# A vision tower on one core: the average's kernel made at the program's beginning, the gather written out over 128 rows, the places loaded in two pieces

## What is computed

```python
logits = jnp.einsum('bsd,de->bse', x, gate_weight)
affinity = jax.nn.softmax(logits, axis=-1).transpose(0, 2, 1)
gating, index = jax.lax.top_k(affinity, k)                       # k = 8 of 65 tokens
x_in = jnp.take_along_axis(x[:, None, :, :], index[..., None], axis=2)
h = jax.nn.gelu(jnp.einsum('bekd,edh->bekh', x_in, w1) + b1[None, :, None, :])
x_e = jnp.einsum('bekh,ehd->bekd', h, w2) + b2[None, :, None, :]
...
def step(h, xt):
    h = p_coeff[None] * xt[:, :, None] + q_coeff[None] * h
    return (h, jnp.sum(gamma[None] * h, axis=-1))           # scanned over the 65 tokens
...
w = jax.nn.softmax(adaptive_weights)
return w[0] * out_attn + w[1] * x_cema
```

## Time and profile before

| | us |
|---|---|
| median of 3 runs | 828.24 (827.29 to 828.71) |
| profiled execution, its own time | 827.36 |
| its span | 825.6 |
| TensorE busy (x8455) | 630.7 |
| VectorE busy (x904) | 504.3 |
| ScalarE busy (x871) | 348.7 |
| GpSimd busy (x254) | 230.8 |

### The profile page before, as it was taken

The page is one execution under the profiler, slowest core; times in us unless marked ns, Lnnn a source line. Parts: engine busy times, 40 slices in busy tenths (PEclk is TensorE's granted clock), DMA queues, the critical chain, the costliest instruction groups (busy, mean ns, idle before and its releaser), DMA issues. The chain is left out here.

```text
span 825.6 us, 21280 instructions
## 1 busy us (share of the span) xinstructions
PE 630.7 (76%) x8455; PEld 513.7 (62%) x8455; DVE 504.3 (61%) x904; ACT 348.7 (42%) x871; POOL 230.8 (28%) x254
## 2 busy tenths in 40 slices
PE   2999999999999996761399867858689999971002
PEld 1888888888888885541394546638567777761001
DVE  0376666666666666427222678759578888855862
ACT  0013444444444444422164333443167888865600
POOL 1263333333333333000000223330235555430001
PEclk9999999999999998665558997775579999995555
DMA  8443333333332300003980440000000000001300
GB/s 358 161 191 119 118 119 117 117 117 117 117 117 117 117 2 2 2 1 106 198 116 0 54 52 0 0 2 0 1 2 4 0 0 0 3 2 53 74 5 4
DMA packets 28659, 55.36 MB, mean 67 GB/s; under 512 B 12274, under 2 KB 25698, under 8 KB 26114
## 3 DMA queue, kind: packets, MB, share of 16 engines
q1 hardware_dynamic: 28515, 54.62, 22.1%
q0 software_dynamic: 96, 0.07, 0.0%
HBM read 48.14 MB, written 6.55 MB: 66 GB/s over the span
## 5 line engine op out<-in xcount | busy, mean ns | idle before, releaser
L375 PE MATMUL a_bank<-a_x,a_tok_w 128*128 128x256 f32 (+1 forms) x608 | 150.6, 390 | 15.7 <-DVE a_ht L555 15.7
L375 PEld LDWEIGHTS a_bank<-a_x,a_tok_w 128*128 128x128 f32 (+1 forms) x608 | 113.1, 192 | 37.3 <-DMA tables<-in_tables 15.7
L124 POOL TENSOR_TENSOR a_qt<-a_qp,data 128x512 f32<-128x512 f32 x64 | 71.8, 1153 | 2.1 <-POOL a_qp L617 1.6
L617 POOL TENSOR_TENSOR a_qp<-a_rope 128x260 f32<-128x260 f32 x16 | 11.7, 733 | 175.5 <-DVE a_rope L499 175.5
L282 ACT ACTIVATE a_at<-a_bank 65x256 f32<-65x256 f32 x128 | 38.9, 390 | 26.8 <-PE a_bank L259 26.8
L493 DVE SCALAR_TENSOR_TENSOR a_ht<-a_bank,data 128x256 f32<-128x256 f32 x16 | 7.7, 484 | 64.5 <-PE a_bank L375 64.5
L1449 POOL TENSOR_TENSOR b_e<-b_e,b_inv 128x585 f32<-128x585 f32 (+1 forms) x32 | 35.4, 1108 | 22.6 <-DVE b_inv L1299 22.6
L259 PE MATMUL a_bank<-a_mix,a_e 64*65 64x64 f32 x1024 | 41.5, 237 | 0.0
L259 PEld LDWEIGHTS a_bank<-a_mix,a_e 64*65 64x65 f32 x1024 | 36.9, 149 | 4.1 <-issue 3.4
L910 POOL COPY s_ycp<-yout 128x512 f32<-128x512 f32 (+1 forms) x16 | 11.5, 726 | 97.6 <-POOLq L829 93.5
L195 ACT ACTIVATE a_e<-a_e 128x390 f32<-128x390 f32 (+1 forms) x48 | 24.3, 510 | 33.2 <-DVE a_e L175 33.2
(11 more groups left out here) (251 smaller groups left out, 1520.2 us busy)
## 6 DMA issues: line engine op xcount, KB each, us to landing
a_x<-in_x SPq DMA_DIRECT2D x16, 2304.0 KB, 7.9
lag_rows<-r_kernel SPq DMA_DIRECT2D x1, 4192.5 KB, 38.8
lags<-lag_rows SPq DMA_DIRECT2D x1, 2112.5 KB
base<-places SPq DMA_DIRECT2D x1, 2080.0 KB
out<-e_plain SPq DMA_DIRECT2D x16, 130.0 KB
expert_weights<-in_w SPq DMA_DIRECT2D x2, 1024.0 KB, 5.9
a_tok_w<-in_tok_w SPq DMA_DIRECT2D x1, 1152.0 KB, 6.7
data<-in_data SPq DMA_DIRECT2D x1, 910.5 KB, 4.7
```

The costliest lines, as they stand in the source:

```text
L124: nc.gpsimd.tensor_tensor(qt[:, b * BLOCKS * P:(b + 1) * BLOCKS * P].rearrange("p (c h i) -> p c h i", i=qb, h=HEADS), wide(by_image[:, b, ...
L375: mm = nc.tensor.matmul(banks[0][:, 0:GP], w[0:rows, k * DIM:(k + 1) * DIM], x[p][0:rows, k * GP:(k + 1) * GP], start=(k == 0), stop=(k == ...
```

## The change

1. **The average's kernel.** `prepare_average` is split. Its first part, now `average_kernel`, stands at the head of VectorE's program of the first block, behind a wait for `data` alone (`S.data_in`, which takes the place of one half of `S.setup`) and ahead of the wait for the tables. SP stores `lag_rows` at the end of its program of the first block, behind the last load of `x`, and waits for it there. The rest, `blend_of_branches`, stays in the second block; the two operations on `adapt` and that on `wo_bv` move behind the subtraction of the peak.
2. **The gather.** `R.h_tok` gets 128 partitions; GpSimd clears partitions 64 to 127 at the program's beginning, and row 64 is written again with every group. TensorE reads `h_tok` itself, so the copies to `tok` go. There are four `pick` of 128 partitions, whose upper 64 GpSimd clears in the second block and of which VectorE writes 65, and four PSUM banks. The loops are written out. The product is 128 rows by 128 columns instead of 65 by 128; what is added is zero.
3. **The places.** SP waits for `places` only, and loads `place_all` for groups 0 to 3 and then for groups 4 to 15. Only then it stores `gates`, and reads both back into `rows`. TensorE turns `rows` behind the gather instead of ahead of it, and VectorE copies the result out at its end.

```diff
+            sp.wait_ge(S.kernel_done, 1)
+            sp.dma_start(R.lag_rows, wide(kernel[:, :].unsqueeze(1), [P, TOKENS, 2 * TOKENS - 1])).then_inc(R.lags_saved, 16)
+            sp.wait_ge(R.lags_saved, 16)
...
-            dve.wait_ge(S.setup, 32)
+            dve.wait_ge(S.data_in, 16)
...
+            average_kernel(nc, dve, R, (powers, square, kernel), then, S)
+            dve.wait_ge(S.setup, 16)
...
+            nc.gpsimd.memset(R.h_tok[HALF:, :, :], 0.0).then_inc(S.zeroed, 1)
...
-        tok = [sb(f"tok{i}", [TOKENS, GI * DIM]) for i in range(2)]
-        pick = [sb(f"pick{i}", [TOKENS, GI * P]) for i in range(2)]
+        pick = [sb(f"pick{i}", [P, GI * P]) for i in range(4)]
...
-            nc.vector.tensor_scalar(wo_bv[:, :], D("wo1"), D("bv1"), None, ALU.mult).then_inc(S.bv_spread, 1)
             then(nc.vector.tensor_reduce(peak[:, :], logits, AX.X, ALU.max))
             nc.vector.tensor_tensor(logits, logits, over(peak), ALU.subtract).then_inc(S.shifted, 1)
+            nc.vector.tensor_scalar(wo_bv[:, :], D("wo1"), D("bv1"), None, ALU.mult).then_inc(S.bv_spread, 1)
...
-            prepare_average(nc, dve, R, (powers, square, kernel, small), then, S, banks[3])
+            blend_of_branches(nc, dve, R, small, then, S, banks[3])
+
+            dve.wait_ge(S.padded, 4)
+            for g in range(GROUPS):
+                dve.wait_ge(S.loaded if g < FIRST else S.loaded_rest, 16)
+
+                wait_past(dve, S.gathered, g - 3)
+                nc.vector.tensor_scalar(pick[g % 4][0:TOKENS, :], place_all[:, g, :], T("iota_p", TOKENS), None,
+                                        ALU.is_equal).then_inc(S.picked, 1)
...
+            for g in range(GROUPS):
+                pe.wait_ge(S.picked, g + 1)
+
+                wait_past(pe, S.stored, g - 3)
+                for b in range(GI):
+                    mm = nc.tensor.matmul(banks[4 + g % 4][:, b * P:(b + 1) * P], R.h_tok[:, g, b * DIM:(b + 1) * DIM],
+                                          pick[g % 4][:, b * P:(b + 1) * P], start=True, stop=True)
+                mm.then_inc(S.gathered, 1)
...
+            for i in range(4):
+                nc.gpsimd.memset(pick[i][HALF:, :], 0.0).then_inc(S.padded, 1)
...
+            sp.wait_ge(S.saved, 16)
+            flat_places = R.places.rearrange("(g n) k -> g (n k)", g=GROUPS)
+            for some, done in ((slice(0, FIRST), S.loaded), (slice(FIRST, GROUPS), S.loaded_rest)):
+                sp.dma_start(place_all[:, some, :], wide(flat_places[some].unsqueeze(0),
+                                                         [TOKENS, some.stop - some.start, GI * P])).then_inc(done, 16)
             sp.dma_start(R.gates.rearrange("(t p) k -> p t k", p=P), best[:, :, :]).then_inc(S.saved, 16)
             sp.wait_ge(S.saved, 32)
```

More of the change, by code:

```diff
@@ L549, in save_logits, with then @@
                 nc.vector.tensor_copy(R.logits[:, g, :], logit_bank).then_inc(S.log_saved, 1)
-            dve.wait_ge(S.setup, 32)
+            dve.wait_ge(S.data_in, 16)
+            count = [0]
+            def then(ins):
+                count[0] += 1
+                ins.then_inc(S.step, 1)
+                dve.wait_ge(S.step, count[0])
+            average_kernel(nc, dve, R, (powers, square, kernel), then, S)
+            dve.wait_ge(S.setup, 16)
             nc.vector.tensor_tensor(mix[:, :], D("w_post"), T("same_query"), ALU.mult)
@@ L642, in _, with average_kernel @@
                     save(g - 1)
-def prepare_average(nc, dve, R, A, then, S, bias_bank):
-    powers, square, kernel, small = A
+def average_kernel(nc, dve, R, A, then, S):
+    powers, square, kernel = A
     D = lambda name: R.data[:, DATA[name][0]:DATA[name][0] + DATA[name][1]]
-    nc.vector.tensor_reduce(small[:, 0:1], D("adapt"), AX.X, ALU.max).then_inc(S.adapt, 1)
-    dve.wait_ge(S.adapt, 1)
-    nc.vector.tensor_scalar(small[:, 1:3], D("adapt"), small[:, 0:1], None, ALU.subtract).then_inc(S.adapt, 1)
     then(nc.vector.memset(kernel[:, :], 0.0))
@@ L686, in route_and_gather @@
         TILES = IMAGES * EXPERTS0 // P
[L687 to L692, removed]
+        FIRST = 4
+        banks = [ctx.enter_context(nc.psum_tensor(f"r_bank{i}", [P, 512], F32)) for i in range(8)]
+        S = named_semaphores(R.ctx, nc, "r_", "step shifted exp_done probs turned best saved loaded loaded_rest read ident_done "
+                  "picked gathered stored adapt bv_spread value_bias padded")
+        small = sb("small", [P, 8])
         wo_bv = sb("wo_bv", [P, DIM])
@@ L795, in _ @@
             mm.then_inc(S.ident_done, 1)
-            for i in steps(pe, 0, GROUPS // 2):
-                for p in range(2):
-                    pe.wait_ge(S.copied, 2 * i + p + 1)
-                    pe.wait_ge(S.picked, 2 * i + p + 1)
-                    wait_past(pe, S.stored, 2 * i + p - 1)
-                    for b in range(GI):
-                        mm = nc.tensor.matmul(banks[p][:, b * P:(b + 1) * P], tok[p][:, b * DIM:(b + 1) * DIM],
-                                              pick[p][:, b * P:(b + 1) * P], start=True, stop=True)
-                    mm.then_inc(S.gathered, 1)
+        @block.gpsimd
+        def _(pool):
+            for i in range(4):
+                nc.gpsimd.memset(pick[i][HALF:, :], 0.0).then_inc(S.padded, 1)
         @block.sync
```

70 lines of the change are left out of this document (29 added, 41 removed).

## The result

The changed kernel takes **809.56 us** (median of 4 runs, 807.47 to 811.73) beside 828.48 us for the kernel before on the same chip: a ratio of **0.9776**, 95% interval 0.9759 to 0.9794. The forecast was 808.0 us, range 803 to 820.5. The profiled execution took 807.47 us with a span of 805.7, the one before 827.36 with 825.6. The execution that was profiled was the shortest of the four. A second set on another chip, with a second trace (experiment 5), gave 809.07 us and 0.9769 (0.9753 to 0.9786).

What follows compares the result with a forecast made beforehand. The second block was taken as bound by a chain: VectorE, the places' load, then TensorE's 27.80 us half-clock gather. 827.4 - 18.0 - 2.2 = 807.2 us profiled, plus 0.9 for the median: 808.0 us, range 803 to 820.5.

Steps and rivals of the forecast that it cites:

- Ahead of the load: Second block before the places' load: first piece issued at 389.28 instead of 391.43, 2.15 us earlier.
- The first piece: Load of places for groups 0 to 3: takes 5.1 us, lands at 394.4, TensorE starts at 395.0.
- The second piece: Load for groups 4 to 15: 13.0 us, between bounds 9.9 and 14.1; lands at 402.3, group 4 at 402.9.
- The second rival: Places' load is quick, second piece lands at 395.6, TensorE never waits: 801.7 us; chance 0.09.
- The clock's rise: Gather: full clock 4.4 us after group 4 starts, at 407.3; TensorE ends at 415.7.
- kept over the wait: Gather: a clock risen before the wait for the second piece and held; worth another 2.2 us, given nothing.
- The block's end: Second block: about 0.9 us of tail after the gather, end at 416.6 instead of 434.6, -18.0 us.
- The experts: Experts' products start at full clock: 4.4 us at half clock become 2.2, -2.2 us.
- The beginning: First block: moved powers (5.4 us) and GpSimd's clearing (7.2 us) hide behind the wait for tables, cost 0.
- `lag_rows`: Store in the first block: issued at about 271 behind the last `x`, lands by 310, hidden.
- The third rival: First block: `lag_rows` holds up the last `x`, losing 26 us: 834 us; chance 0.03.
- Later blocks: Blocks after the experts: unchanged, though clock changes may fall otherwise by a microsecond or two either way.

Runs made afterwards that it cites:

- experiment 5: The changed kernel, unaltered, run a second time on another chip for a second trace: 809.07 us, ratio 0.9769.
- the move without `lag_rows` beside the load: Kernel before, with only the average's kernel and the store of `lag_rows` moved to the first block: 829.03 us, ratio 0.9995.
- experiments 2 and 3: Kernel before with the average's kernel and `lag_rows` store moved to the first block: alone 829.03 us, with a 128-row gather too 821.96 us.
- The bridge: Changed kernel plus six unread 128x128 products of ones between experts and scatter, where TensorE was idle: 807.28 us, ratio 0.9744.
- five pieces with warm-up: Changed kernel with places loaded in five pieces, plus twelve unread products of ones on TensorE before the gather: 800.70 us, ratio 0.9673.
- the two moves together: Kernel before with a 128-row gather (through ScalarE's copies) and the average's kernel and `lag_rows` moved to the first block: 821.96 us, ratio 0.9925.

## Why the prediction was right, step by step

- **Ahead of the load.** First piece issued at 389.28 forecast, 389.21 measured; the store lands, and the piece goes, 2.2 us behind it. The operations on `wo_bv` and `adapt` lie in VectorE's wait for ScalarE.
- **The first piece** was given 5.1 us and took 4.4 (4.6 in the second trace, 4.8 to 5.0 in the three other kernels with two pieces). TensorE started at 394.11, forecast 395.0. The forecast was 0.9 us too late, the 0.7 of the piece and the rest from the pick's start.
- **The second piece** was given 13.0 us and took 13.1: group 4 at 402.82, forecast 402.9. The choice against the bound of 9.9 us, which the move without `lag_rows` beside the load later denied (13.8 us), was the one on which the forecast hung. The second rival (a quick load) asked for the same thing and fell with it.
- **The clock's rise** is the step that was mis-sized. I let it rise only in group 4. It rose 3.9 us after the first product of all, inside groups 0 to 3, and was kept over the wait of 3.0 us, so that the 12 groups took 11.0 us where I had 12.8. My own 4.4 us, counted from the first product at 395.0, would have put the rise at 399.4, ahead of the wait; I had no row for what a wait does to the clock and left the term at nothing. This is the "kept over the wait" for which I gave nothing. In the second trace the rise was early as well, the clock was lost after the wait, and the gather ended at 415.6, where the forecast had 415.7. So both outcomes occur in the same program, 1.8 us apart, and the sum had the dearer one.
- **The block's end.** Forecast -18.0 us; the experts' start moved by -20.1 and -18.4. From the gather's end to it 1.0 us, forecast 0.9.
- **The experts** gave -2.2, forecast -2.2.
- **The beginning** cost nothing: GpSimd's clearing took 6.92 us (forecast 7.2), the powers were done by 12.8 where I had 11, the tables came at 15.2, and TensorE started at 15.83 against 15.74. The 1.8 us are in one row, a copy of 16 columns that took 2.00 us and ended at 7.86, right behind GpSimd's clearing of the token store:

```profile
0.90 6.92 POOL L647 MEMSET h_tok<- 64x8192 f32 x1
5.86 2.00 DVE L671 COPY a_square<-data 128x16 f32<-128x16 f32 x1
```

The same copy took 0.17 us in the two kernels of experiments 2 and 3 that have the powers here and no such clearing, and 1.86 us, again until 7.85, in the second trace. The clear and the product ahead of it (5.44 to 5.82) ran beside the clearing at their usual length. So the clearing held up VectorE for one operation, and the wait for the tables hid it.
- **`lag_rows`** issued at 271.22 landed 38.1 us later, 65 us ahead of the block's end; the last `x` was not late. The third rival did not happen. The fit to which the second rival was compared (the Trainium skill, DMA: Bandwidth & Descriptors, "Anatomy of one DMA") is one for transfers that GpSimd issues, and this load is issued by SP, so that the 6.9 us need not hold for it.
- **Later blocks** had one term too small. I allowed a microsecond or two either way; the scatter lost **3.2 and 3.1 us** in the two traces. The bridge showed what the loss hangs on: with experts at the full clock from their first product and 1.75 us without work between experts and scatter, the clock fell some 2 us into the scatter, for over 6 us, in six of seven traces, and with products in that gap in none of three. In each of the four traces whose experts began cold, the fall came later (10.5 to 11.2 us after the start in three, 27.4 in the kernel before), and the stage took 86.8 to 86.9 us. It came later once with warm experts too (five pieces with warm-up), so the early fall is likely and not certain. Why experts that began cold carry the clock over the same gap stays open.

That the sum closed within 0.3 us in the first trace is luck, since its errors nearly cancel: 2.1 us more from the gather than forecast, 3.2 us given back in the scatter, 0.7 gained later. In the second the gather's stage was near the forecast and the loss stood alone, less 1.0 us in later blocks: 807.2 us of span against the 805.4 that the sum amounts to (807.2 less the 1.8 us around a span). The second trace is the more typical one: its execution took 808.98 us beside a median of 809.07, while the first took 807.47 beside 809.56, so the median lies 1.6 us above the forecast of 808.0.

What the change consists of, by the ratios: the two moves together 0.75%, each alone nothing; the order of the transfers and the gather without copies, written out, another 1.0%; cutting the load the last 0.5%. Taking the rows back from the changed kernel loses 1.0%, more than both moves together gave on the kernel before, so these parts do not simply add.

## What to carry to other kernels

When two things end a block at nearly the same time, here a gather at half clock and a store of 39 us, removing either alone measures as nothing: the sum has to name what is late next, and the pair has to be tried together. Where TensorE waits for a load on a stage's only path, cut the load into pieces by the order of use; here the first piece cost 4 to 5 us, and part of the rest hid behind work. Behind a stage that has become faster, look at the beginning of the next one for what it gave back.

## What the runs showed that I had not expected

- Rows of zeros are not idle ballast to the clock: 65 rows stayed at 1.2 GHz through 20.8 busy us, 128 rows, 63 of them zeros, were at 2.4 GHz 3.9 us after the start. In the eight traces in which the gather itself began cold with 128 rows, the rise came 2.9 to 5.6 us after its first product.
- Whether a short wait costs the clock is not told by its length: it was kept over 3.02 and 3.08 us, and lost after 2.45, 3.42 and 4.53 us. When it is lost it shows 0.4 to 1.1 us after work has begun again, and stays low for 3.4 us in these three. The Trainium skill (TensorE: Matmul & The Clock Gate, "What's actually happening") says that what watches TensorE's activity runs free and is not reset when a kernel starts; that would fit a wait that is sometimes harmless, but no run here controlled it.
- The load of `base`, 2080 KB from one source of 32 KB, took 13.8 to 14.2 us without the 4 MB of `lag_rows` beside it and 14.1 to 14.6 with them.
- In several executions of kernels with the average's kernel at the beginning, the first group of the first block was up to 1.6 us later, its products coming slower until 22 us (first reload of `x` at 26.1 to 27.7 us, against 26.0 and 26.3 in the two traces without the move). The block made it up or not by its end. Whether the move causes it was not tried.
